# Where TensorE does its other work within a half step: between the scores for the maximum and the scores for the exponent, instead of after both

## The chip, the cores and the metric

The kernel runs on one core of a Trainium2 chip. TensorE (PE) multiplies matrices into PSUM, VectorE (DVE) does reductions and elementwise work, ScalarE (ACT) does exponentials and copies, GpSimd (POOL) elementwise work and indirect transfers, SyncE (SP) issues the other transfers. The metric is the device time of one execution in microseconds (us), lower is better; of several runs the median counts.

## What is computed

```python
x = L0_attn_x                                  # 16 batches, 512 tokens, 128 features
mod = (_silu(L0_c) @ L0_wmod)                  # per batch: shift, scale and gate, twice
h = _layernorm(x) * (1 + ca) + sa
q, k, v = h @ Wq.T + bq, h @ Wk.T + bk, h @ Wv.T + bv          # 16 heads of 8
attn = softmax(q @ k.T / sqrt(8))              # per head 512 x 512
x = x + ga * ((attn @ v) @ Wo.T + bo)
h = _layernorm(x) * (1 + cb) + sb
gating = softmax of the two best of 8 experts' scores (h @ gate_w.T)
x = x + gb * sum over the two experts of gating * (silu(h @ wg.T) * (h @ wu.T)) @ wd.T
```

## The kernel before

The attention of the 16 batches comes first, and the mixture of experts behind it, tile by tile. Each engine has one instruction stream, written out by hand and joined to the others by semaphores. A batch `b` is 16 slots `k = 0..15`; four slots make a group `g` of four heads, `hh = k % 4` is the slot within its group, and each slot has two halves, so that a batch has 32 half steps. Each half step handles 1024 scores in each of 128 rows (two heads of 512), twice:

- **Scores for the maximum** (line 824, tile `ps<-k_st,q_st`): two matmuls, for the group that is two groups ahead. DVE takes the row maximum of them (line 1331, `maxes`, one TENSOR_REDUCE a half step).
- **Scores for the exponent** (line 833, `ps<-q_st,k_st`): two matmuls, transposed, for the present group, with the negated maxima as two extra rows of the contraction. ACT takes exp of them into `probs` (line 1039, one ACTIVATE a half step).

PSUM has three areas of two banks for these, taken in turn by both kinds. So the scores for the exponent of half step s may be written when DVE has finished the maximum of half step s-1 (semaphore `maxes_done`), and the scores for the maximum of half step s when ACT has finished the exponent of half step s-2 (`exps_done`).

Once a slot TensorE also multiplies `probs` of the group before with `v_aug` (line 847, four matmuls of float32 that the trace counts as eight, into the bank `PV_BANK`): the **v_aug products**. In the first slot of a group they wait until ACT has copied the last group's result out of that bank (line 1046, `o_aug`, semaphore `pv_taken`); ACT does this copy after the first exponent of the group's first slot. Here `L111` rows in a listing are register arithmetic for the semaphore values inside a loop.

**Other steps** (`misc_at`, names in quotes) go through one shared bank, each filled by TensorE and drained by ACT or DVE before the next is filled: "shift" (the maxima transposed, line 757, drained by DVE at line 1177, then sent by DMA into `q_st`), "o" (line 762, drained at 1182 and 1184), "v" (753), "oT" (765), "y" (768, drained by ACT into `z`, line 1028, which waits for the small transfer of `prm_t`), "x1" (771), "hT" (746), "q" (748), "k" (750), "h2T" (775, waits for the second norm on POOL), "score" (778) and "where" (788 to 792) of the router, and "count" once. In a slot of the kernel before TensorE does: maximum, exponent, maximum, exponent, the first other step if there is one, the v_aug products, the second other step.

DVE has two reductions in a slot, and between them, at places written in the tables `NORM_AT` and `ROUTER_AT`, the small steps of the second layer norm and of the router. POOL splits q and k of the batch after next into three bfloat16 parts (lines 1515 to 1521) when ACT has drained "q" and "k" (line 1018), then does the second norm (1531 to 1538) and the scatters (1545). SP stores the parts of k to DRAM, and loads them back rearranged as `q_st` and `k_st` (line 518), behind which stand the loads of `x_r` and `prm_t` (488, 489). The new stacks are first read at k = 8. The last slots of batch 16 on, without any scores (`LATE`), are interleaved with the first tiles of the experts.

## Time and profile before

| | |
|---|---|
| median of 3 runs | 1455.21 us (1453.88 to 1474.65) |
| the profiled execution | 1465.6 us, its span 1463.7 us |
| mean granted TensorE clock | 0.879 of full speed |
| busy TensorE, DVE, ACT, POOL | 1097.3, 978.5, 784.1, 528.8 us |
| row maxima (line 1331), 512 times | 613.6 us, 1219 ns each |
| exponents (line 1039), 512 times | 523.1 us, 1023 ns each |
| first and last maximum | 51.5 and 1151.9 us |
| first and last exponent | 72.3 and 1177.3 us |

The span runs from the first to the last instruction; the whole execution is 1.9 us longer. The profiled execution took 0.7% more than the median of the other runs. The attention fills the time from about 51 to 1178 us, the experts fill the rest. Busy shares are means over both.

### The profile page before, as it was taken

To read this page: it belongs to the slowest core of one execution; us is meant where nothing else is said; L and a number is where in the kernel's file an instruction comes from. 1 tells how busy PE (TensorE), PEld (TensorE's weight loads), DVE (VectorE), ACT (ScalarE), POOL (GpSimd) and SP (SyncE) were. 2 spreads that over 40 slices of the span, in tenths; PEclk is the share of its full clock that TensorE was granted. 3 is DMA by queue.
4 is the path that set the end of the run, shared out by engine and by line. 5 is a ranking of instruction groups with operands and counts; after the bars stand their busy time and mean duration, and the time that the engine had idled before them with its cause. 6 is when DMAs were issued, how large, how long until landed. Compare 5 with 4: busy or idle time off the path is not lost.

```text
span 1463.7 us, 24448 instructions
## 1 busy us (share of the span) xinstructions
PE 1097.3 (75%) x6826; PEld 481.6 (33%) x6827; DVE 978.5 (67%) x2158; ACT 784.1 (54%) x1228; POOL 528.8 (36%) x591
## 2 busy tenths in 40 slices
PE   4477777767776878777877776878777788899981
PEld 2112222222222222222222222222222268798981
DVE  7567778686767675768675867675768554445555
ACT  3256756565555555555454655555555655455540
POOL 3112031423142323241405142323142157787754
PEclk9669999798789887889688989897889899999996
DMA  8132130314031212030303031213030042335677
GB/s 246 48 98 68 41 107 13 116 33 124 12 117 41 87 40 87 29 99 19 108 12 116 12 116 40 87 33 94 14 107 22 17 111 75 102 96 150 188 193 199
DMA packets 143146, 121.46 MB, mean 83 GB/s; under 512 B 20709, under 2 KB 133458, under 8 KB 139986
## 3 DMA queue, kind: packets, MB, share of 16 engines
q1 hardware_dynamic: 134354, 102.50, 24.4%
q0 software_dynamic: 8704, 17.97, 3.7%
q8 instruction: 32, 0.52, 0.1%
q14 instruction: 56, 0.46, 0.1%
HBM read 66.07 MB, written 53.76 MB: 82 GB/s over the span
## 4 chain that ended last, share of the span: by engine, by line
PE 47%; DVE 23%; issue 11%; DMA 6%; POOL 4%; SPq 4%; ACT 4%; DVEq 0%; ACTq 0%; POOLq 0%
PE ps L847 18%; DVE maxes L1331 17%; PE ps L833 6%; PE ps L824 4%; PE ps L896 3%; PE ps L762 3%; PE ps L913 2%; POOL ys_d L1584 2%; DMA k_st<-k_parts_d 2%; ACT probs L1039 2%; PE ps L768 1%; PE ps L905 1%; PE ps L748 1%; ACT o_aug L1046 1%; PE ps L778 1%
## 5 line engine op out<-in xcount | busy, mean ns | idle before, releaser
L1331 DVE TENSOR_REDUCE maxes<-ps 128x2 f32<-128x1024 f32 x512 | 613.6, 1219 | 177.4 <-PE ps L824 157.1
L1039 ACT ACTIVATE probs<-ps 128x1024 f32<-128x1024 f32 x512 | 523.1, 1023 | 342.9 <-PE ps L833 342.2
L833 PE MATMUL ps<-q_st,k_st 50*128 50x512 bf16 x1024 | 219.1, 427 | 253.3 <-DVE maxes L1331 236.6
L847 PE MATMUL ps<-probs,v_aug 128*32 128x512 f32 x2048 | 321.1, 704 | 13.4 <-ACT o_aug L1046 13.3
L1515 POOL TENSOR_TENSOR q_parts<-q,one 128x512 bf16<-128x512 f32 x16 | 16.6, 1035 | 713.0 <-ACT q L1018 713.0
L824 PE MATMUL ps<-k_st,q_st 48*128 48x512 bf16 x1024 | 224.5, 436 | 23.1 <-DMA k_st<-k_parts_d 18.9
L833 PEld LDWEIGHTS ps<-q_st,k_st 50*128 50x128 bf16 x1024 | 50.8, 97 | 405.4 <-DVE maxes L1331 375.3
L1545 POOL DMA_INDIRECT xs_d<-h,rows_o x128 | 123.4, 964 | 36.9 <-issue 36.3
L1460 DVE COPY probs<-ps 88x256 f32<-88x256 f32 x144 | 60.4, 419 | 100.7 <-PE ps L905 93.8
L824 PEld LDWEIGHTS ps<-k_st,q_st 48*128 48x128 bf16 x1024 | 53.3, 101 | 181.8 <-issue 95.4
L913 PE MATMUL ps<-wd_t,probs 88*128 x576 | 93.6, 286 | 0.1
L1584 POOL DMA_INDIRECT ys_d<-probs,k_st x72 | 71.2, 988 | 24.5 <-ACT probs L1096 11.9
L913 PEld LDWEIGHTS ps<-wd_t,probs 88*128 88x128 f32 x576 | 76.9, 194 | 4.8 <-issue 0.7
L1584 POOL DMA_INDIRECT ys_d<-probs,q_st x72 | 70.7, 981 | 17.8 <-POOL gone L1583 7.4
L896 PE MATMUL ps<-wg_t,probs 128*128 x288 | 73.2, 336 | 2.8 <-DVE probs L1464 2.2
L1086 ACT COPY probs<-ps 128x128 f32<-128x128 f32 x143 | 37.9, 265 | 67.2 <-PE ps L889 65.7
L847 PEld LDWEIGHTS ps<-probs,v_aug 128*32 128x32 f32 x2048 | 43.6, 114 | 76.5 <-issue 55.9
L896 PE MATMUL ps<-wu_t,probs 128*128 x288 | 67.7, 317 | 0.0
L905 PE MATMUL ps<-ident,probs 128*88 128x128 f32 x288 | 56.4, 278 | 9.9 <-DVE probs L1464 8.9
L1182 DVE RECIPROCAL o_rs<-ps 128x16 f32<-128x16 f32 x64 | 16.5, 258 | 65.2 <-PE ps L762 65.2
L762 PEld LDWEIGHTS ps<-ident,o_aug 128*128 128x128 f32 x256 | 32.9, 165 | 67.9 <-issue 57.5
L1464 DVE TENSOR_TENSOR probs<-probs,ps 128x176 f32<-128x176 f32 x144 | 46.5, 323 | 10.2 <-ACT probs L1090 9.8
(209 smaller groups left out, 1398.4 us busy)
## 6 DMA issues: line engine op xcount, KB each, us to landing
q_st<-q_parts_d SPq DMA_DIRECT2D x32, 384.0 KB
k_st<-k_parts_d SPq DMA_DIRECT2D x32, 384.0 KB
q_parts_d<-q_parts SPq DMA_DIRECT2D x16, 384.0 KB, 2.6
k_parts_d<-k_parts SPq DMA_DIRECT2D x16, 384.0 KB
probs<-ys_d SPq DMA_DIRECT2D x24, 256.0 KB, 4.8
...
```

The lines of the kernel that those rows point to most:

```text
L762: mm = pe.transpose(misc[:, P * t:P * (t + 1)], o_aug[g % 2][:, P * t:P * (t + 1)], ident[:, :])
L824: mm = pe.matmul(ps[:, 2 * area_of(2 * step) + side, :], q_st[bs % 2][rows, js, P * t:P * (t + 1)], k_st[bs % 2][rows, js, :], start=True, ...
L833: mm = pe.matmul(ps[:, 2 * area_of(2 * step + 1) + side, :], k_st[b % 2][rows, j, P * t:P * (t + 1)], q_st[b % 2][rows, j, :], start=True, ...
L847: mm = pe.matmul(ps[VW * i:VW * (i + 1), PV_BANK, :], v_aug[bp % 2][:, hh, GROUP * gp + i, :], probs[:, gp % 2, i, S * hh:S * (hh + 1)], s ...
L896: mm = pe.matmul(ps[:, GU_BANK + m % 2, INTER * i:INTER * (i + 1)], x_t[m % 2], w[:, :, :].rearrange("p c h -> p (c h)")[:, bass.ds(e * IN ...
L905: mm = pe.transpose(ps[0:HALF, HT_BANK, P * i:P * (i + 1)], hid[m % 2][:, HALF * i:HALF * (i + 1)], ident[:, :])
L913: mm = pe.matmul(ps[:, Y_BANK + m % 2, 0:D], hid_t[m % 2][:, P * i:P * (i + 1)], wd_t[:, bass.ds(e * 2 + i, 1), :].rearrange("p a d -> p ( ...
L1039: act.activation(probs[:, g % 2, pair_at:pair_at + 2, S * t:S * (t + 1)], ps[:, 2 * area:2 * area + 2, :], ACT.Exp, scale=SCALE).then_inc( ...
L1331: dve.tensor_reduce(maxes[g % 2][:, :, hh // 2, tile:tile + 1], ps[:, 2 * area:2 * area + 2, :], AX.X, ALU.max).then_inc(maxes_done, 1)
L1460: dve.tensor_copy(hid_t[(m - 1) % 2], ps[0:HALF, HT_BANK, 0:2 * P]).then_inc(hidt_taken, 1)
L1545: pool.indirect_dma_start(xs_d, bass.IndirectOffsetOnAxis(ap=rows_o[:, v:v + 1], axis=0), h2[n % 2][:, v // QT, v % QT, :], None).then_inc ...
L1584: pool.indirect_dma_start(ys_d, bass.IndirectOffsetOnAxis(ap=x_in[m % SLOTS][:, D + 1:XW].bitcast(U32), axis=0), y_out[m % SLOTS], None).t ...
```

## The change

In each half step TensorE now does the scores for the maximum, then one piece of other work, then the scores for the exponent. The two halves of a slot divide the pieces: the v_aug products in one half (the second in a group's first slot, the first in the other three), the other steps in `half` 0 or 1. "score" moves from k = 6 to k = 8, "where" from 13 to 12, "count" from 12 to 14. ACT and DVE drain in the order of the halves: ACT drains a step ahead of the exponent of the same half, DVE behind the maximum of the same half. `ROUTER_AT` moves the router's first 14 steps six places later and its last 13 four places earlier, and `LATE` is two slots shorter.

```diff
-LATE = [(NB, k) for k in range(GROUP, NH)] + [(NB + 1, k) for k in range(NH)] + [(NB + 2, k) for k in range(2)]
+LATE = [(NB, k) for k in range(GROUP, NH)] + [(NB + 1, k) for k in range(NH)]
-COUNT_AT = (NB - 1, 12)
+COUNT_AT = (NB - 1, 14)
...
-    if not end and (b, k) == COUNT_AT:
-        step = ("count", 0, 1)
-    elif not end:
-        step = {4: ("h2T", b - 2, NB), 6: ("score", b - 2, NB), 13: ("where", b - 2, NB)}.get(k)
+    if not half:
+        step = ("count", 0, 1) if (b, k) == COUNT_AT else {
+            4: ("h2T", b - 2, NB), 8: ("score", b - 2, NB), 12: ("where", b - 2, NB)}.get(k)
...
                             mm.then_inc(scores_ready, 1)
+                        if half == (hh == 0):
+                            weigh_values(b, g, hh, d)
+                        misc_steps(b, k, half, d)
                         if exps:
...
                             mm.then_inc(st_ready, 1)
-                        if half == 1:
-                            misc_steps(b, k, 0, d)
-                    if 0 <= s - 1 < NS:
...
-                        if hh == QT - 1:
-                            mm.then_inc(pv_ready, 1)
-                    misc_steps(b, k, 1, d)
+
+            def weigh_values(b, g, hh, d):
...
```

On ACT, and on DVE:

```diff
                     for half in range(2):
                         t, step = 2 * (hh % 2) + half, 2 * k + half
+                        other = misc_at(b, k, half)
+                        if other and other[0] in ("hT", "q", "k", "v", "oT", "y", "h2T"):
+                            misc_drain(*other, d)
                         if 0 <= s < NS:
...
-                    step = misc_at(b, k, 1)
-                    if step and step[0] in ("hT", "q", "k", "v", "oT", "y"):
-                        misc_drain(*step, d)
...
-            ROUTER_AT = ([BATCH_TILES + 27 + i for i in range(14)]
-                         + [BATCH_TILES + 53 + i for i in range(13)])
+            ROUTER_AT = ([BATCH_TILES + 33 + i for i in range(14)]
+                         + [BATCH_TILES + 49 + i for i in range(13)])
```

On TensorE, an inner slot of a group (k = 5 of a batch), before:

```order
L824 MATMUL ps<-k_st,q_st 128x512 [waits exps_done]
L824 MATMUL ps<-k_st,q_st 128x512
L833 MATMUL ps<-q_st,k_st 128x512 [waits maxes_done]
L833 MATMUL ps<-q_st,k_st 128x512
L824 MATMUL ps<-k_st,q_st 128x512 [waits exps_done]
L824 MATMUL ps<-k_st,q_st 128x512
L833 MATMUL ps<-q_st,k_st 128x512 [waits maxes_done]
L833 MATMUL ps<-q_st,k_st 128x512
L847 MATMUL ps<-probs,v_aug 32x512 x4
L762 MATMUL ps<-ident,o_aug 128x128 [waits pv_taken,misc_drained]
L762 MATMUL ps<-ident,o_aug 128x128 x3
```

and the same slot now (line 825 is the old 824, 837 the old 833, 852 the old 847, 763 the old 762):

```order
L825 MATMUL ps<-k_st,q_st 128x512 [waits exps_done]
L825 MATMUL ps<-k_st,q_st 128x512
L852 MATMUL ps<-probs,v_aug 32x512 x4
L837 MATMUL ps<-q_st,k_st 128x512 [waits maxes_done]
L837 MATMUL ps<-q_st,k_st 128x512
L825 MATMUL ps<-k_st,q_st 128x512 [waits exps_done]
L825 MATMUL ps<-k_st,q_st 128x512
L763 MATMUL ps<-ident,o_aug 128x128 [waits pv_taken,misc_drained]
L763 MATMUL ps<-ident,o_aug 128x128 x3
L837 MATMUL ps<-q_st,k_st 128x512 [waits maxes_done]
L837 MATMUL ps<-q_st,k_st 128x512
```

The v_aug products and the "o" transposes have moved from behind the second scores for the exponent to ahead of the first and of the second.

On TensorE, the first slot of a group (k = 4), from its first scores for the exponent on, before:

```order
L833 MATMUL ps<-q_st,k_st 128x512 [waits maxes_done,shift_stacked]
L833 MATMUL ps<-q_st,k_st 128x512
L824 MATMUL ps<-k_st,q_st 128x512 [waits exps_done]
L824 MATMUL ps<-k_st,q_st 128x512
L833 MATMUL ps<-q_st,k_st 128x512 [waits maxes_done]
L833 MATMUL ps<-q_st,k_st 128x512
L775 MATMUL ps<-ident,h_0 128x128 [waits h2_ready,misc_drained]
L775 MATMUL ps<-ident,h_0 128x128 x3
L847 MATMUL ps<-probs,v_aug 32x512 [waits misc_drained,pv_taken,exps_done]
L847 MATMUL ps<-probs,v_aug 32x512 x3
L757 MATMUL ps<-identb,shift 32x128 [waits shift_ready,misc_drained]
```

and the whole of that slot now:

```order
L825 MATMUL ps<-k_st,q_st 128x512
L776 MATMUL ps<-ident,h_0 128x128 [waits h2_ready,misc_drained]
L776 MATMUL ps<-ident,h_0 128x128 x3
L837 MATMUL ps<-q_st,k_st 128x512 [waits maxes_done,shift_stacked]
L837 MATMUL ps<-q_st,k_st 128x512
L825 MATMUL ps<-k_st,q_st 128x512 [waits exps_done]
L825 MATMUL ps<-k_st,q_st 128x512
L852 MATMUL ps<-probs,v_aug 32x512 [waits misc_drained,pv_taken,exps_done]
L852 MATMUL ps<-probs,v_aug 32x512 x3
L758 MATMUL ps<-identb,shift 32x128 [waits shift_ready,misc_drained]
L837 MATMUL ps<-q_st,k_st 128x512 [waits maxes_done]
L837 MATMUL ps<-q_st,k_st 128x512
```

"h2T" stands ahead of the first scores for the exponent, and the wait for `pv_taken` ahead of the second.

On ACT, at the end of slot 7 and the start of slot 8, before:

```order
L1006 ACTIVATE x_n<-x_a,prm_a 128x128 [waits misc_filled]
L111 REGISTER_ALU
L111 REGISTER_ALU [waits misc_filled]
L1028 ACTIVATE z<-ps,prm_t 128x512 [waits xr_loaded]
L111 REGISTER_ALU
L1039 ACTIVATE probs<-ps 128x2x512 [waits st_ready]
L111 REGISTER_ALU
L111 REGISTER_ALU [waits pv_ready]
L1046 COPY o_aug<-ps 128x512 [waits misc_filled]
```

and now (1032 is the old 1028, 1046 the old 1039, 1010 the old 1006, 1053 the old 1046):

```order
L1032 ACTIVATE z<-ps,prm_t 128x512 [waits xr_loaded]
L111 REGISTER_ALU
L1046 ACTIVATE probs<-ps 128x2x512 [waits st_ready]
L111 REGISTER_ALU
L111 REGISTER_ALU [waits xa_loaded]
L1010 ACTIVATE x_n<-x_a,prm_a 128x128 [waits misc_filled]
L111 REGISTER_ALU
L1046 ACTIVATE probs<-ps 128x2x512 [waits st_ready]
L111 REGISTER_ALU
L111 REGISTER_ALU [waits pv_ready]
L1053 COPY o_aug<-ps 128x512 [waits misc_filled]
```

The drain of "y", with its wait for a transfer, now stands ahead of the last exponent of slot 7.

## Rows read from the trace of the kernel before

**Rows 1.** The waits, 324.8 to 1058.6 us and 300 to 1000: total, times, longest.

```profile
PE ps L833 <- DVE maxes L1331: 160.1, 157, 5.5
DVE maxes L1331 <- PE ps L824: 99.1, 63, 3.2
...
DVE maxes L1331 <- issue: 16.5, 8, 2.6
```

**Rows 2.** ACT's copy of "k", and two stretches from one such copy to another.

```profile
L1018 ACT ACTIVATE k<-ps,bias x16: 687/687/688, 24.1 to 1058.6; 128x512 f32<-128x512 f32 x16
324.80:1058.60 733.80, 554.03 (x3242) 171.79 (x3240) 512.98 (x1002) 402.62 (x481) 221.54 (x211) 0.85 0.21 65
132.60:191.90 59.30, 42.99 (x304) 12.79 (x306) 45.69 (x73) 39.58 (x46) 8.90 (x9) 1.00 0.25 70
```

**Rows 3.** The timeline, one inner slot (k = 5): start, length, engine, line, idle before.

```profile
565.85 0.39 PE L824 MATMUL ps<-k_st,q_st 48*128 48x512 bf16 x2
...
566.08 0.38 PE L833 MATMUL ps<-q_st,k_st 50*128 50x512 bf16 x2
...
566.28 2.36 DVE L1331 TENSOR_REDUCE maxes<-ps 128x2 f32<-128x1024 f32 x2
...
566.50 1.02 ACT L1039 ACTIVATE probs<-ps 128x1024 f32<-128x1024 f32 x1 [0.94 <-PE ps L833]
...
567.57 0.39 PE L833 MATMUL ps<-q_st,k_st 50*128 50x512 bf16 x2 [0.89 <-DVE maxes L1331]
...
567.88 1.06 PE L847 MATMUL ps<-probs,v_aug 128*32 128x512 f32 x8
...
568.88 0.66 PE L762 MATMUL ps<-ident,o_aug 128*128 128x128 f32 x4
...
569.47 0.39 PE L824 MATMUL ps<-k_st,q_st 48*128 48x512 bf16 x2
```

**Rows 4.** The timeline: the copy at a group's start, and "v", the longest step.

```profile
560.83 1.16 PE L753 MATMUL ps<-w_t,h_t 128*128 128x128 f32 x8
...
600.26 0.58 ACT L1046 COPY o_aug<-ps 128x512 f32<-128x512 f32 x1
...
600.99 1.07 PE L847 MATMUL ps<-probs,v_aug 128*32 128x512 f32 x8 [0.40 <-ACT o_aug L1046]
```

**Rows 5.** Busy us (instructions) of PE, PEld, DVE, ACT, POOL; clock; DMA.

```profile
582.20:617.60 35.40, 27.58 (x161) 8.37 (x160) 26.41 (x63) 20.48 (x25) 3.06 (x3) 0.85 0.04 12
...
558.30:572.60 14.30, 10.77 (x78) 4.34 (x75) 10.41 (x13) 9.40 (x11) 4.79 (x5) 0.98 0.35 116
572.60:582.30 9.70, 9.22 (x34) 2.43 (x36) 3.38 (x9) 3.31 (x5) 0.00 (x0) 0.50 0.00 1
```

**Rows 6.** The same stretch for the row maxima alone (DVE, clock, DMA).

```profile
582.20:617.60 35.40, 19.20 (x16) 0.85 0.04 12
```

**Rows 7.** The timeline around a fall of the clock, TensorE.

```profile
571.67 1.36 PE L778 MATMUL ps<-gw_t,h_t 128*128 128x8 f32 x8
...
576.27 0.63 PE L833 MATMUL ps<-q_st,k_st 50*128 50x512 bf16 x2
576.70 0.63 PE L824 MATMUL ps<-k_st,q_st 48*128 48x512 bf16 x2
...
578.34 1.94 PE L847 MATMUL ps<-probs,v_aug 128*32 128x512 f32 x8
580.21 2.08 PE L768 MATMUL ps<-o_t,w_t 128*128 128x512 f32 x2
```

**Rows 8.** From "k" to the stacks: timeline, landing of `prm_t` (min, median, max).

```profile
692.08 0.69 ACT L1018 ACTIVATE k<-ps,bias 128x512 f32<-128x512 f32 x1 [1.10 <-PE ps L750]
...
696.78 1.16 POOL L1521 TENSOR_TENSOR k_parts<-rest,k_parts 128x512 bf16<-128x512 f32 x1
...
705.87 0.36 SPq L489 DMA_DIRECT2D prm_t<-prm_d x1
...
DMA to landing us min/median/max: 2.5/14.6/16.5
```

45 lines of the change are left out of this document (23 added, 22 removed).

## The prediction

> **What bounds the kernel now.** I read the page first for the shares, then the waits over ten steady batches, then the timeline of single slots, then the granted clock stretch by stretch. No engine is full: the ten batches between the copies of "k" take 733.8 us, 73.4 a batch, and in them TensorE is busy for 554 us and DVE for 513 [rows 2]. The waits show that the two wait for each other: TensorE stands 160.1 us for a row maximum before scores for the exponent, and DVE stands 99.1 us for TensorE before a maximum [rows 1]. One slot shows how. The scores for the maximum start at 565.85, the reduction at 566.28 (0.43 later), and the second scores for the exponent, which need its area, only at 567.57; TensorE stands 0.89 us. Only then come the v_aug products (1.00 us, 567.88 to 568.88) and the "o" transposes (0.59), and the next scores for the maximum start at 569.47. DVE has finished its two reductions at 568.64 and has nothing to read until 569.9 [rows 3]. So a slot is a loop: reduction 1.24, scores, products, other step, scores, 3.62 us for this one, although TensorE has only 4 x 0.22 + 1.00 + 0.59 = 2.5 us of work in it and DVE 2 x 1.18 = 2.4 and a drain.
>
> **The change, an inner slot.** Nothing is removed or added; each product takes what it took. The products and the other step now stand where TensorE waited. With a pair of scores at 0.22 (566.08 less 565.85 is 0.23) the order is scores 0.22, products 1.00, scores 0.22, scores 0.22, step 0.1 to 1.1, scores 0.22: 2.0 to 3.0 us. Three loops remain. DVE: 2.36 for two reductions, plus small steps. TensorE: those 2.0 to 3.0. ACT: scores for the exponent to the start of the exponent 0.42 (566.08 to 566.50), the exponent 1.02 [rows 3], release 0.05, the next scores for the maximum 0.22, then the products 1.00 before the next scores of that half: 2.7. A step that ACT drains adds its drain ahead of the exponent; "k" takes 0.69 [rows 2]. I take 2.75 for a slot with a short step and 3.1 for one with the longest ("v", 1.16 with its tail) [rows 4].
>
> **A group's first slot.** Here the products wait for the `o_aug` copy, which follows the first exponent. Before, TensorE was waiting for a maximum at that time anyway, so that only 0.40 us showed [rows 4]. Now the wait is in front of the second scores for the exponent. Counted from the first scores for the exponent: 0.42 + 1.02 + 0.58 (the copy) + 0.05, products 1.00, "shift" 0.15, scores 0.22 = 3.45 until the next scores for the maximum, 3.9 until DVE has something to reduce. The first slot also has to wait for the last maximum of the group before. Laid end to end in that way, a group of four slots with few small DVE steps comes to 3.5 + 2.5 + 2.9 + 3.2 = 12.1 us, and one with "h2T", "oT" and "y" to 12.9, since "h2T" is drained ahead of that exponent. The first half of a batch: **25 us**. Queued behind the waiting products are the "shift" transposes and the scores; who waits for them is DVE. A price for the wait from both sides: 0.40 as now, or all of the 2.07 us from scores to the copy's end; I use the second less what DVE still has to reduce.
>
> **The second half of a batch** (k = 8 to 15) is where the router's and the norm's small steps lie. DVE was busy for 26.4 us of it, 19.2 of them in 16 reductions [rows 5, 6], so the 47 others took 7.2, 0.15 each. The new table moves 7 more router steps in (those at k = 6 and 7, and in the next batch's slot 0): 7 x 0.15 = 1.1. That is 27.5 us of DVE, which is now the bound; two group starts leave it idle for 0.65 us each, and dependent steps and POOL's splits running beside it add some 2: **31 us**. "score" and "where" move to a group's first slot, where their 1 us stands beside the wait for the last maximum and costs nothing; if that wait were gone they would cost 2 us a batch.
>
> **Transfers.** They keep their length while the slots get shorter. "k" was drained at 692.08, POOL's split of it ended at 697.94, and `prm_t`, last in the row behind the stacks, was issued at 705.87 and takes 14.6 us: 28.4 us after "k" [rows 8]. SP was held there by a "shift" drain which will come earlier; I work out 27.2. "y" is drained at k = 7, some 24 us after "k", and ACT has to have `prm_t` for it, now ahead of an exponent: a wait of 2 to 3 us, which delays the second scores of k = 8: **2 us** a batch. Bounds: 0 (in the few batches with a quick landing, 2.5 us) and 4.4 (all of 28.4). The stacks themselves land just before k = 8 on that count. POOL's second norm, which "h2T" at k = 4 waits for, is five operations of about a split's 1.16 [rows 8] behind the split: 6 us more, some 11 us after the batch's start where 12.1 is early enough. No cost, with 1 us to spare.
>
> **Once a loop turn**, of two batches, DVE waits for its own instructions, 16.5 us in five turns [rows 1]: **1.5 us** a batch, unchanged.
>
> **The clock.** At the low level, 1.2 GHz against 2.4, products take 1.87 (578.34 to 580.21) and a pair 0.43 [rows 7]. The mean of 0.85 over the ten batches means 30% of the time at the low level [rows 2]. It fell at 572.6 right after "score", eight columns a matmul, though TensorE had been busy for 10.8 of the 14.3 us before, at 0.98, and it rose 9.7 us later [rows 5, 7]. A slot without other work needs 4 x 0.43 + 1.87 = 3.6 us there, with one 4.6 to 5.5, so TensorE is the bound and a slot costs some 1.2 more than laid out above. With TensorE a little denser, but "score" and "where" next to the new waits, I take a quarter of the time: about three slots, **3.5 us**. The Trainium skill speaks against this term: "TensorE: Matmul & The Clock Gate", section "What's actually happening", lets the clock fall only after an idle window. By that rule the term would be near 0. The trace does not agree: what precedes the fall at 572.6 is three quarters work.
>
> **The sum.** 25 + 31 + 2 + 1.5 + 3.5 = 63 us a batch against 73.4: 10.4 saved in each of ten batches, 104. The three batches ahead of them (192.2 us from 132.6 to 324.8, 64.1 each) have less DVE work and a clock of up to 1.00 [rows 2]: 7.3 each, 22. Batch 0's last eight slots and batches 14 and 15: 17. The start is bound by transfers and the experts' part by its own steps; the two LATE slots less let the second map be made two tiles earlier, which nobody waits for: 0. In all 143 us of the profiled execution's 1465.6, 1322.6; the median stood 0.7% below that execution, so **1313 us**.
>
> **Rivals.**
> *A, the clock stays up.* If a denser TensorE keeps 2.4 GHz, the 3.5 us go too: 14 x 3.5 = 49 less, 1264. This is what the Trainium skill's rule on idle windows, named above, would give. For it: the batch from 132.6 to 191.9 ran at 1.00 throughout. Against: that batch has no "score" and no "where".
> *B, ACT becomes the bound.* Steps are drained ahead of exponents, and copies stand before products. If each of eight drains a batch (0.7) delays the loop in full, it costs 5.6 us, less what is in the slots above: 69 a batch, 1313 + 14 x 6 = 1397. For it: the ACT loop of 2.7 is longer than DVE's 2.36. Against: ACT was busy for 403 of 734 us [rows 2].
> *C, the clock stays down: slower.* At 1.2 GHz throughout, a batch is 16 x 3.6 = 57.6 of scores and products and twice 10.5 of other steps (at the full clock four "shift" of 0.15, four "o" of 0.59, ten others of 0.6 to 1.1), 80 us with the loop turn: 6.6 more than now, 1455 + 14 x 6.6 = 1547. It would come about if new waits, at each group's start and before k = 8, make the clock fall again whenever it has risen. It decides against the change when the low level holds for (73.4 - 59.5) / (80 - 59.5) = 68% of the time, against 30 now. Against: total waiting shrinks.
> *D, nothing gained.* The moved work doesn't lie under the wait, because something else ends last at each scores for the exponent: POOL's chain from "k" through split, store and load to k = 8 stretches with the traffic. To hold a batch at 73 it would have to take 10 us more than the 28.4 seen: 1455.
>
> **Chances.** The forecast, with batches of 61 to 66 us, 0.45; A 0.22; B, or a transfer that waits by some us more, 0.20; C 0.06; D 0.07. A measurement of this kernel tells about 2% from no change. Faster by over 2%: 0.45 + 0.22 + 0.20 less a little for a weak B = 0.86; within 2% 0.08; slower 0.06. The range takes in A with a batch at 57.5 us, the bare sum of both halves and the loop turn (1313 - 14 x 5.5 = 1236), and B (1397) with a little for a longer wait at k = 8: 1235 to 1405.
>
> **What the profile after would show.** Batches of about 63 us between copies of "k". TensorE's wait for maxima before scores for the exponent down to a third of 160; DVE's wait for scores mostly at group starts, about 1 us each. A new wait of the products for `o_aug`, 1.3 to 1.6 us, 60 times. ACT waiting for `prm_t` before `z` for 2 to 3 us a batch. A clock of 0.86 to 0.92. The time of one product, reduction and exponent unchanged. I am wrong if the clock's mean leaves these bounds, if ACT's queue holds the exponents longer, or if the stacks come after their slot.

## The result

| | before | after |
|---|---|---|
| median of 4 runs | 1458.72 us (1453.88 to 1474.65) | **1400.58 us** (1395.41 to 1405.94) |
| profiled execution, its span | 1465.6, 1463.7 us | 1395.4, 1393.6 us |
| mean granted TensorE clock | 0.879 | 0.853 |

The ratio is **0.9584, 95% interval 0.9497 to 0.967**: faster by 58 us of medians (70.1 us between the two spans), where 143 were forecast. Here and below a median counts all runs, while a ratio is formed from the runs in the faster of the two states in which a kernel is found, and no clock is given for e7 and e10, whose profiled executions fell in the slower one. The reduction now has line 1332, and the other steps keep their tiles.

The page of the changed kernel: busy time of the engines, and two of the costliest groups.

```profile
PE 1113.4 (80%) x6826; PEld 477.0 (34%) x6827; DVE 981.3 (70%) x2158; ACT 779.6 (56%) x1228; POOL 528.5 (38%) x591
...
L1332 DVE TENSOR_REDUCE maxes<-ps 128x2 f32<-128x1024 f32 x512 | 622.3, 1222 | 136.5 <-PE ps L825 119.3
L852 PE MATMUL ps<-probs,v_aug 128*32 128x512 f32 x2048 | 341.9, 746 | 78.4 <-ACT o_aug L1053 63.5
```

The counts and the length of a reduction are as before. What changed is who waits. The products (line 852) now stand 63.5 us for the `o_aug` copy over the whole run. The stretches between copies of "k" (columns as in [rows 2]):

```profile
129.60:185.90 56.30, 46.57 (x304) 12.97 (x304) 45.82 (x74) 39.14 (x46) 8.93 (x9) 0.94 0.25 74
315.90:982.90 667.00, 548.37 (x3242) 164.03 (x3242) 513.77 (x1003) 399.88 (x480) 221.37 (x211) 0.83 0.24 72
```

The copies themselves, in the timeline grouped by tile (how many; shortest, middle and longest in ns; first and last start):

```profile
L1022 ACT ACTIVATE k<-ps,bias x14: 687/687/688, 129.6 to 982.9; 128x512 f32<-128x512 f32 x14
```

Ten batches take 667.0 us where [rows 2] had 733.8: 66.7 each instead of 73.4, with the same instructions (x3242 on TensorE) and a mean clock of 0.83 instead of 0.85. TensorE was idle for 179.8 us of them before (733.80 less 554.03) and is for 118.6 now. The time of the whole went like this:

| stretch | before | after | saved | forecast |
|---|---|---|---|---|
| start to the copy of "k" at 129.6 | 132.6 | 129.6 | 3.0 | 0 |
| three batches | 192.2 | 186.3 | 5.9 | 22 |
| ten batches | 733.8 | 667.0 | 66.8 | 104 |
| the rest | 405.1 | 410.7 | -5.6 | 17 |

The waits in the ten batches (total, times, longest), to be set beside [rows 1]:

```profile
DVE maxes L1332 <- PE ps L825: 64.1, 114, 1.7
DVE shift_t L1178 <- PE ps L758: 57.7, 32, 2.4
...
PE ps L852 <- ACT o_aug L1053: 39.8, 31, 1.6
...
PE ps L837 <- DVE maxes L1332: 22.4, 20, 4.0
PEld ps L789 <- DVE top L1241: 18.7, 10, 1.9
...
PE ps L789 <- DVE top L1241: 13.7, 10, 1.4
...
ACT z L1032 <- DMA prm_t<-prm_d: 5.2, 3, 2.8
```

TensorE's wait for a maximum fell from 160.1 to 22.4 us. The main mechanism is there. Two other waits of TensorE have come up: 39.8 us for `o_aug`, 31 times and up to 1.6 us (forecast at each group's start; 6.7 us before), and 13.7 for `top`, 1.4 us each time, once a batch. The second is not in the prediction at all. Line 789 is "where"; its weight load (PEld) waits 1.9 us.

DVE's wait for scores fell from 99.1 to 64.1 us, but the one for "shift", which TensorE now does behind the waiting products, rose to 57.7. In the same ten batches before it was:

```profile
DVE shift_t L1177 <- PE ps L757: 20.2, 29, 1.7
```

**An inner slot and a group's first slot.** The timeline of TensorE over k = 4 and the beginning of k = 5 (start, length):

```profile
605.74 0.39 PE L837 MATMUL ps<-q_st,k_st 50*128 50x512 bf16 x2
606.01 0.39 PE L825 MATMUL ps<-k_st,q_st 48*128 48x512 bf16 x2
607.97 1.07 PE L852 MATMUL ps<-probs,v_aug 128*32 128x512 f32 x8 [1.57 <-ACT o_aug L1053]
608.85 0.22 PE L758 MATMUL ps<-identb,shift 128*32 128x128 bf16 x1
609.00 0.39 PE L837 MATMUL ps<-q_st,k_st 50*128 50x512 bf16 x2
609.22 0.38 PE L825 MATMUL ps<-k_st,q_st 48*128 48x512 bf16 x2
609.53 1.06 PE L852 MATMUL ps<-probs,v_aug 128*32 128x512 f32 x8
610.53 0.39 PE L837 MATMUL ps<-q_st,k_st 50*128 50x512 bf16 x2
610.76 0.38 PE L825 MATMUL ps<-k_st,q_st 48*128 48x512 bf16 x2
611.07 0.65 PE L763 MATMUL ps<-ident,o_aug 128*128 128x128 f32 x4
611.66 0.39 PE L837 MATMUL ps<-q_st,k_st 50*128 50x512 bf16 x2
612.04 0.39 PE L825 MATMUL ps<-k_st,q_st 48*128 48x512 bf16 x2
```

The slot of k = 5 runs from 609.22 to 612.04, 2.82 us, with hardly a gap (the forecast was 2.75; [rows 3] had 3.62). At k = 4 the products wait 1.57 us for the copy; from the first scores for the exponent, 605.74, to the next scores for the maximum, 609.22, it is 3.48 us (forecast 3.45). Both units of the sum were right. What the 3.45 leaves out is what stands ahead of the first scores for the exponent.

**The slot of k = 8**, where "score" (line 779) has been put:

```profile
616.84 1.23 DVE L1332 TENSOR_REDUCE maxes<-ps 128x2 f32<-128x1024 f32 x1 [0.31 <-PE ps L825]
...
618.80 1.06 PE L779 MATMUL ps<-gw_t,h_t 128*128 128x8 f32 x8 [0.41 <-ACT z L1032]
619.79 0.39 PE L837 MATMUL ps<-q_st,k_st 50*128 50x512 bf16 x2
```

The last reduction of the group before ends at 618.07, so there is no wait for a maximum left to hide anything under. "score" waits 0.41 us for ACT's drain of "y" and takes 0.99, and the scores for the exponent start right behind it. From the scores for the maximum, which start at 618.01, it is 1.78 us to them. At k = 4 it is the same with "h2T": scores for the maximum 604.49, last reduction over at 604.52, "h2T" from 605.16 on, scores for the exponent 605.74.

**The slot of k = 12** is the surprise. The timeline of three engines:

```profile
632.03 0.38 PE L825 MATMUL ps<-k_st,q_st 48*128 48x512 bf16 x2
...
633.59 0.14 DVE L1241 TENSOR_TENSOR top<-top 128x4 f32<-128x4 f32 x1
...
633.79 0.64 PE L789 MATMUL ps<-route,tri 128*128 128x32 f32 x2 [1.37 <-DVE top L1241]
...
634.24 1.43 PE L791 MATMUL ps<-route,ones 128*128 128x24 f32 x6
...
635.52 0.61 PE L793 MATMUL ps<-before,ones 128*128 128x32 f32 x2
...
636.07 0.61 PE L837 MATMUL ps<-q_st,k_st 50*128 50x512 bf16 x2
...
636.72 1.02 ACT L1046 ACTIVATE probs<-ps 128x1024 f32<-128x1024 f32 x1 [3.45 <-PE ps L837]
...
638.36 1.93 PE L852 MATMUL ps<-probs,v_aug 128*32 128x512 f32 x8 [1.26 <-ACT o_aug L1053]
```

After the scores for the maximum (632.03) TensorE comes to "where", whose input is the router's step on DVE that ends at 633.73. It stands 1.37 us for it, then "where" takes 2.3 us, and only then (636.07) come the scores for the exponent, which ACT had been waiting for since 633.3. Its `o_aug` copy is thereby late as well, and the products wait another 1.26. The clock, as stretches from the same place:

```profile
604.00:632.00 28.00, 23.75 (x169) 7.77 (x170) 22.88 (x41) 21.49 (x28) 1.92 (x2) 1.00 0.16 55
632.00:634.00 2.00, 0.63 (x5) 0.21 (x2) 2.00 (x8) 1.15 (x2) 0.00 (x0) 0.83 0.00 0
634.00:642.00 8.00, 6.74 (x31) 2.84 (x35) 4.42 (x15) 2.56 (x4) 0.00 (x0) 0.50 0.01 2
```

It was 1.00 (2.4 GHz) until 632, through the wait at k = 4 too. The 0.83 of the next 2.00 us means the low level for their last 0.7, so it fell at about 633.3, while TensorE stood for `top` (until 633.79); then it is 0.50 (1.2 GHz) for at least 8 us.

**Mean slot lengths.** From scores for the maximum to the next, worked out from the timeline and averaged over the ten batches (k = 0 has the loop turn in it):

| k | 0 | 1 | 2 | 3 | 4 | 5 | 6 | 7 | 8 | 9 | 10 | 11 | 12 | 13 | 14 | 15 |
|---|---|---|---|---|---|---|---|---|---|---|---|---|---|---|---|---|
| before | 6.6 | 5.4 | 3.6 | 4.2 | 3.9 | 3.6 | 6.2 | 5.3 | 3.6 | 3.8 | 3.9 | 5.3 | 3.6 | 5.4 | 4.8 | 4.2 |
| after | 7.1 | 4.3 | 2.9 | 3.2 | 5.3 | 3.3 | 2.8 | 3.3 | 5.8 | 3.2 | 2.8 | 3.4 | 8.4 | 4.0 | 3.1 | 3.6 |

The twelve slots that don't begin a group gained 15.6 us a batch, and the four that do (0, 4, 8, 12) lost 8.8. The net 6.8 is what the stretches show.

### The profile page after: what moved, and what is told of

Read it like the earlier page. It is cut to its first block, busy times and chain, and to the rows that moved or that the text cites. A ratio compares the mean times of both kernels' runs of the same rounds, so it can differ in the third digit from the quotient of the medians.

```text
span 1393.6 us, 24448 instructions
## 1 busy us (share of the span) xinstructions
PE 1113.4 (80%) x6826; PEld 477.0 (34%) x6827; DVE 981.3 (70%) x2158; ACT 779.6 (56%) x1228; POOL 528.5 (38%) x591
## 4 chain that ended last, share of the span: by engine, by line
PE 41%; issue 16%; DMA 12%; DVE 11%; SPq 6%; ACT 6%; POOL 6%; DVEq 1%; ACTq 0%; POOLq 0%
PE ps L852 15%; PE ps L837 7%; DMA prm_t<-prm_d 5%; DVE maxes L1332 5%; PE ps L825 5%; ACT probs L1046 3%; PE ps L900 3%; PE ps L917 2%; POOL ys_d L1584 2%; DMA k_st<-k_parts_d 2%; ACT o_aug L1053 2%; PE ps L763 2%; DMA k_parts_d<-k_parts 1%; PE ps L909 1%; PE ps L779 1%
## 5 line engine op out<-in xcount | busy, mean ns | idle before, releaser
L1332 DVE TENSOR_REDUCE maxes<-ps 128x2 f32<-128x1024 f32 x512 | 622.3, 1222 | 136.5 <-PE ps L825 119.3
L852 PE MATMUL ps<-probs,v_aug 128*32 128x512 f32 x2048 | 341.9, 746 | 78.4 <-ACT o_aug L1053 63.5
L1460 DVE COPY probs<-ps 88x256 f32<-88x256 f32 x144 | 60.4, 420 | 101.1 <-PE ps L909 93.5
L1178 DVE COPY shift_t<-ps 32x128 bf16<-32x128 bf16 x64 | 13.5, 211 | 91.3 <-PE ps L758 90.9
L1531 POOL TENSOR_TENSOR h<-x_s,ln 128x512 f32<-128x512 f32 x16 | 16.6, 1039 | 89.2 <-DMA row<-row_d 48.0
```

The lines of the kernel that those rows point to most:

```text
L852: mm = pe.matmul(ps[VW * i:VW * (i + 1), PV_BANK, :], v_aug[bp % 2][:, hh, GROUP * gp + i, :], probs[:, gp % 2, i, S * hh:S * (hh + 1)], s ...
L1332: dve.tensor_reduce(maxes[g % 2][:, :, hh // 2, tile:tile + 1], ps[:, 2 * area:2 * area + 2, :], AX.X, ALU.max).then_inc(maxes_done, 1)
L1460: dve.tensor_copy(hid_t[(m - 1) % 2], ps[0:HALF, HT_BANK, 0:2 * P]).then_inc(hidt_taken, 1)
```

## The experiments

"A batch" is the distance of the thirteen copies of "k" divided by 13 (71.2 us before, 65.6 after). Ratios are to the kernel before on the same chip.

| run | edit | median | ratio [95%] | a batch | clock |
|---|---|---|---|---|---|
| e1_router_early | after + router two steps a place | 1365.4 | 0.9425 [0.9335, 0.9514] | 63.8 | 0.873 |
| e2_copy_early | after + `o_aug` copy early | 1329.7 | 0.9185 [0.9137, 0.9232] | 61.4 | 0.884 |
| e3_prm_early | after + `x_r`, `prm_t` ahead of the stacks | 1405.9 | 0.971 [0.9636, 0.9785] | 66.4 | 0.848 |
| e4_drain_behind | after + ACT drains behind the exponent | 1448.2 | 0.9987 [0.9942, 1.0033] | 69.1 | 0.831 |
| e5_router_copy | e1 and e2 together | 1306.8 | 0.8946 [0.8871, 0.902] | 60.0 | 0.892 |
| e6_products_only | before + only the products moved | 1382.4 | 0.9484 [0.9396, 0.9573] | 64.6 | 0.903 |
| e7_before_copy_early | before + copy early | 1440.4 | 0.9856 [0.9772, 0.994] | 70.8 | |
| e8_router_copy_prm | e5 + `prm_t` alone ahead | 1314.8 | 0.8984 [0.887, 0.9097] | 60.4 | 0.889 |
| e9_steps_only | after, products back at the slot's end | 1336.3 | 0.9187 [0.9093, 0.9281] | 61.9 | 0.913 |
| e10_router_copy_xr | e5 + both loads a batch ahead | 1280.9 | 0.8723 [0.8608, 0.8839] | 58.9 | |
| e11_old_places | after with the tables of before | 1420.5 | 0.9749 [0.9652, 0.9847] | 66.9 | 0.851 |
| e12_filled_waits | after + useless matmuls in the `o_aug` wait | 1401.7 | 0.963 [0.9532, 0.9727] | 65.7 | 0.866 |
| e13_steps_router | e9 + e1 (disturbed, see there) | 1485.8 | 0.9451 [0.9373, 0.9529] | 68.0 | 0.859 |
| e14_steps_copy | e9 + copy early (beside e13) | 1436.7 | 0.9127 [0.906, 0.9194] | 64.0 | 0.880 |
| e15_steps_all | e10, products at the end (beside e13) | 1438.3 | 0.9139 [0.9079, 0.92] | 64.6 | 0.873 |
| e16_all_one_chip | e10 again | 1271.6 | 0.8764 [0.8691, 0.8837] | 58.2 | 0.901 |
| e17_steps_all_one_chip | e15 again, beside e16 | 1291.4 | 0.8898 [0.8822, 0.8974] | 59.5 | 0.926 |
| e18_steps_router_copy | e17, loads in their old place | 1302.4 | 0.8957 [0.8865, 0.9049] | 60.1 | 0.916 |

### The wait of "where" for the router (e1)

```diff
-            ROUTER_AT = ([BATCH_TILES + 33 + i for i in range(14)]
+            ROUTER_AT = ([BATCH_TILES + 33 + i // 2 for i in range(14)]
...
-                        if place in ROUTER_AT:
-                            router_step(ROUTER_AT.index(place), n, d)
+                        for i, p in enumerate(ROUTER_AT):
+                            if p == place:
+                                router_step(i, n, d)
```

> The changed kernel, with the router's first 14 steps two to a place (places 33 to 39 of the batch in place of 33 to 46), so that the last of them is done on DVE long before TensorE reaches "where" at k = 12. Theory 1, group starts: the changed kernel loses in the first slot of a group what it gains in the others (k = 12 takes 8.4 us where it took 3.6 before), and part of that is the 1.9 us that the weight load of "where" waits for DVE's step 13 (L1241). Then k = 12 drops to about 6.5 and a batch by 2 us: 1373 us, ratio to the kernel before 0.941. Theory 2, clock: "where" makes the clock fall wherever it stands, the slot stays above 7.5 and the whole moves by under 10 us (ratio 0.952 or more).

35 us less than the changed kernel by medians, 23 by the two ratios. No wait for `top` is left; slot 12 went from 8.4 to 5.9 us and the clock up. The wait for `o_aug` is untouched, as the waits of e1 between 310 and 960 us show:

```profile
PE ps L852 <- ACT o_aug L1053: 39.8, 29, 1.6
```

So the wait of "where" costs 2.5 us in its slot, and 1.8 a batch, since slots 8 to 10 got a little longer. With the wait gone slot 12 is still 2.3 us longer than before (5.9 against 3.6): "where" itself and the wait for `o_aug` stand in it.

### The wait of the products for `o_aug` (e2, e5, e12, e7)

e2 lets ACT copy behind the first exponent of a group's last slot, in which the products end; the products then no longer find the bank full.

```diff
-                        if hh == 0 and half == 0 and 0 <= s - 2 < NS:
+                        if hh == GROUP - 1 and half == 0 and 0 <= s - 1 < NS:
...
-                            wait(act, pv_ready, lambda b: NG * b + g - 1, b, d)
+                            wait(act, pv_ready, lambda b: NG * b + g, b, d)
...
-                            act.copy(o_aug[g % 2][:, :], ps[:, PV_BANK, :]).then_inc(pv_taken, 1)
+                            act.copy(o_aug[(g + 1) % 2][:, :], ps[:, PV_BANK, :]).then_inc(pv_taken, 1)
```

> The changed kernel, with ACT's copy of the v_aug products (o_aug) behind the first exponent of a group's last slot, where the products are finished, in place of behind the first exponent of the next group's first slot. Theory 1, group starts: the products' wait for that copy, 1.3 to 1.6 us at each group start, goes; what is late next is the last maximum of the group before, 0.3 to 0.5 us behind it. Some 1 us for each of 60 groups: 1340 us, ratio 0.92. Theory 2, clock: the waits are what makes the clock fall, so its mean rises over 0.88 as well and the time is 1325 or less. Rival, transfers: the batch is held by the chain from k through split, store and load (prm_t is on the chain that ended last for 5% of the span); the slots only wait elsewhere, and the time stays above 1385.

71 us less than the changed kernel by medians, 58 by the ratios: the k = 4 slot went from 5.3 to 3.1 us. Something else then came up. The waits of e2 between 310 and 960 us:

```profile
ACT z L1032 <- DMA prm_t<-prm_d: 25.8, 9, 7.3
...
PE ps L825 <- DMA k_st<-k_parts_d: 18.3, 8, 6.5
```

These are the transfers that the prediction spoke of; slots 7 and 8 (5.0 and 5.7 us on average) are where they are waited for. e5 puts e1's and e2's edits together.

> The changed kernel with both edits: the router's first 14 steps two to a place, and the o_aug copy behind the first exponent of a group's last slot. Theory 1, group starts: the two losses are separate (1.9 us before "where", 1.1 us for each of 60 groups) and add up: 0.9425 and 0.9185 against the change's 0.9584 give 0.9584 - 0.016 - 0.040 = 0.903, 1317 us. Rival, transfers: with the copy early alone k = 7 and 8 already wait for prm_t and for the stacks (4.7 and 5.2 us a slot), and what the router's edit gives comes out there again: 0.915 or more.

94 us less than the changed kernel (93 by the ratios). The sum of the two is 106 by medians and 81 by ratios: two separate waits, that add up. 1306.8 us is near the 1313 that had been forecast for the change itself.

e12 asks whether the wait costs by itself or through the clock: it leaves the wait and fills it with five matmuls of 48 rows, whose result nobody reads.

```diff
+                        if hh == 0 and half == 1 and exps and 0 <= s + 1 < NS:
+                            wait(pe, misc_drained, lambda b: at["shift", NG * b + g + 1], b, d)
+                            for _ in range(5):
+                                pe.matmul(misc, k_st[b % 2][0:SHIFT, j, P * t:P * (t + 1)], q_st[b % 2][0:SHIFT, j, :],
+                                          start=True, stop=True)
                         if half == (hh == 0):
                             weigh_values(b, g, hh, d)
```

> The changed kernel with five useless bf16 matmuls of 48 rows by 512 columns into the shared bank before the products in each group's first slot, where TensorE waits 1.3 to 1.6 us for the o_aug copy; 1.1 us of work at the high clock. It computes nothing new; the bank is written again by "shift". Theory 2, the new waits make the clock fall: its mean rises from 0.853 to 0.89 or more and 15 to 40 us go, ratio 0.93 to 0.95. Theory 1, what is lost is the waits themselves and the clock falls at "score" and "where", with few active columns: the mean stays below 0.87, the time within 1% of the changed kernel or up to 10 us longer.

The visible wait is nearly gone (3.6 us in 12 times), slots 4 and 5 stayed at a steady 4.7 and 2.8 us, and the mean clock rose from 0.853 to 0.866. The time did not move (0.963 against 0.9584, with intervals that overlap): slot 12 remained (9.2 us), and the five matmuls take more than the wait wherever the clock is low, 2.34 us at 771.64 against 1.25 at 805.70. So the higher clock alone brought nothing here; how the cost of the wait divides between waiting and clock isn't shown, since the filling adds work of its own.

e7 is the control: the copy early in the kernel before (there `half == 1`, since the products stand at the slot's end).

> The kernel before with the o_aug copy behind the second exponent of a group's last slot. Theory 1: the wait for this copy is new in the changed kernel; before, TensorE stood at most 0.4 us for it, 6.7 us in ten batches, so 5 to 10 us at most go: ratio 0.993 to 1. Rival: the place of the copy is worth much in either order (it keeps ACT free at the group's start): 0.98 or less.

18 us by medians, 21 by the ratio (0.9856, interval 0.977 to 0.994): between the two expectations, and more than the kernel before shows as waiting, 6.7 us in ten batches. The 0.40 us of [rows 4] is one of the long ones, not the mean of 60. Why the copy's place is worth more than its wait stays open. Of what e2 gave back about a third was thus to be had without the change, and the rest goes with the change's own wait.

### The transfers (e3, e8, e10)

e3 moves `load_x_r(b - 1, d)`, the loads of `x_r` and `prm_t`, ahead of `store_parts` and `load_stacks` in SP's stream:

```diff
+                if 0 <= b - 1 < NB:
+                    load_x_r(b - 1, d)
                 if b + 1 < NB:
...
-                if 0 <= b - 1 < NB:
-                    load_x_r(b - 1, d)
```

> The changed kernel, with SP's loads of x_r and prm_t ahead of the stores of k's parts and the loads of the stacks, so that the drain of "y" never waits for prm_t. Theory 1: that wait is 7.2 us in all, so 0 to 10 us less: 1390 to 1401. Rival, transfers: the chain that ended last runs through prm_t for 5% of the span (70 us), and if it really sets the batch, 20 us or more go (1380 or less). It may also cost, if the 256 KB of x_r ahead delay the stacks past k = 8: then a wait of the scores for the maximum for stack_ready appears in the trace.

No gain: in the changed kernel `z` waited only 5.2 us in ten batches, and the stacks, now later, were waited for instead (8.3 us for `k_st` between 310 and 960 us, where the changed kernel has 1.5). e8 repeats it where the transfers do bind, on top of e5, with `prm_t` alone ahead and `x_r` left behind the stacks:

```diff
             def load_x_r(n, d):
 
+                b = batch_of(n, d)
+                sp.dma_start(x_r[:, :, :], x[b].rearrange("(t p) d -> p t d", p=P)).then_inc(xr_loaded, 16)
+
+            def load_prm_t(n, d):
+
                 wait(sp, misc_drained, lambda n: at["x1", n - 1] + 1 if n else 0, n, d)
                 b = batch_of(n, d)
-                sp.dma_start(x_r[:, :, :], x[b].rearrange("(t p) d -> p t d", p=P)).then_inc(xr_loaded, 16)
                 sp.dma_start(prm_t[:, :], prm_d[b]).then_inc(xr_loaded, 16)
...
+                if 0 <= b - 1 < NB:
+                    load_prm_t(b - 1, d)
                 if b + 1 < NB:
```

> The kernel of e5 with SP's small load of prm_t (6 KB) ahead of the stores of k's parts and of the stacks, x_r left behind them. ACT's wait for prm_t before z (25.8 us in 650 with the copy early) goes. Theory, transfers bind only through prm_t: 20 to 30 us less than e5, about 1295. Rival: the stacks land 2 us later than prm_t is wanted, the wait moves from z to the scores for the maximum at k = 8, and under 12 us are gained.

No gain over e5 (0.8984 against 0.8946). The waits of e8 between 310 and 960 us:

```profile
ACT z L1039 <- DMA x_r<-L_attn_x: 23.9, 11, 8.2
...
PE ps L832 <- DMA k_st<-k_parts_d: 17.2, 8, 7.7
```

The semaphore counts both loads, and the last in the row behind the stacks is the late one, whichever it is. e10 issues both a batch earlier, behind `store_x1` and `load_row` of the batch before, as soon as "x1" has freed them:

```diff
-                if 0 <= b - 1 < NB:
-                    load_x_r(b - 1, d)
...
                     load_row(b - 1, d)
+                if 0 <= b < NB:
+                    load_x_r(b, d)
```

> The kernel of e5 with x_r and prm_t loaded a batch earlier, behind the store of x1, where no other transfer runs, in place of behind the stacks. Theory, what is last in the row behind the stacks lands late (with prm_t moved ahead alone, z waited for x_r in its place): z's waits of 25.5 us go, and the scores for the maximum at k = 8 become what waits, for k_st, 1 to 3 us a batch. 10 to 25 us less than e5: 1290, ratio 0.883. Rival: both waits are one chain (from k through split and stacks), nothing is gained: 0.89 or more.

The fastest kernel of the study, 1280.9 us, and 1271.6 as e16. Both loads now land 3.6 us after their issue at the median (3.5 and 3.6 in e16), and `z` waits for no transfer any more. The stacks are still waited for in some batches: 7.6 us in all between 310 and 880 us of e16, up to 6.2 at a time.

### The two halves of the change apart (e6, e9), and ACT's order (e4)

e6 is the kernel before with nothing changed but the products' place: `weigh_values` is called behind the scores for the maximum, in the halves that the change uses.

```diff
                             mm.then_inc(scores_ready, 1)
+                        if half == (hh == 0):
+                            weigh_values(b, g, hh, d)
                         if exps:
```

> The kernel before with one part of the change: only the v_aug products move, to between the scores for the maximum and for the exponent; the other steps, their drains, the tables and LATE stay as they were. Theory 1: inner slots lose the 1.0 us of the products from their loop (3.25 to about 2.4 without another step, 3.62 to 2.9 with "o"), the first slot of each group gains the wait for o_aug (+1.2 us), "where" stands behind the second scores as before and does not wait for DVE: about 12 x 0.8 - 4 x 1.2 = 4.8 us a batch less, 1385 us, ratio 0.95, no worse than the whole change. Rival, that the other steps' place carries most of the gain: 0.975 or more.

The waits of e6 between 310 and 960 us:

```profile
PE ps L853 <- ACT o_aug L1051: 56.3, 35, 2.1
...
PE ps L835 <- DVE maxes L1336: 32.7, 60, 2.9
```

It gains as much as the whole change, with a larger wait for `o_aug`. e9 is the opposite: the steps moved, the products back at the slot's end.

```diff
-                        if half == (hh == 0):
-                            weigh_values(b, g, hh, d)
                         misc_steps(b, k, half, d)
...
                             mm.then_inc(st_ready, 1)
+                    weigh_values(b, g, hh, d)
```

> The changed kernel with the v_aug products back behind the slot's last scores for the exponent; the other steps stay between the two kinds of scores, the tables are the new ones. Theory 1, the products carry the change and bring its loss with them: inner slots keep the products in their loop (3.2 us each, and nothing more for a step), group starts have no wait for o_aug, k = 12 keeps the wait of "where". 12 slots of 3.3 and 4 group starts of about 4.4, two of them 1 to 3 longer, and 1.5 for the loop turn: 64 to 68 us a batch, ratio 0.94 to 0.97. Rival, each part gives half: 0.975 to 0.985.

The waits of e9 between 310 and 930 us:

```profile
PE ps L835 <- DVE maxes L1331: 51.7, 79, 3.4
...
PE ps L851 <- ACT o_aug L1052: 19.7, 26, 1.0
...
PE ps L789 <- DVE top L1240: 2.7, 10, 0.3
```

A miss for both theories, on the good side: 0.9187. The wait for maxima is twice the changed kernel's, but that for `o_aug` is half and that for `top` a fifth. As built, moving the products as well costs 64 us (58 by the ratios).

e4 puts ACT's drains behind the exponent of the same half, the rest as changed (three lines moved behind the exponent):

```diff
-                        other = misc_at(b, k, half)
-                        if other and other[0] in ("hT", "q", "k", "v", "oT", "y", "h2T"):
-                            misc_drain(*other, d)
...
                                            ps[:, 2 * area:2 * area + 2, :], ACT.Exp, scale=SCALE).then_inc(exps_done, 1)
+                        other = misc_at(b, k, half)
+                        if other and other[0] in ("hT", "q", "k", "v", "oT", "y", "h2T"):
+                            misc_drain(*other, d)
```

> The changed kernel, with ACT's drains of the other steps behind the exponent of the same half step instead of ahead of it. Rival B of the prediction (drains ahead of exponents make ACT the bound): eight drains a batch of 0.6 to 0.8 us no longer stand before an exponent, a batch loses 3 us, 1360 or less. Theory 1: inner slots are bound by the loop over the exponent only in part; what is gained there (at most 0.5 us for each of the 8 slots) is lost where the next step waits for the shared bank ("score" behind "y", "h2T" behind "v"): 1390 to 1410.

The waits of e4 between 320 and 960 us:

```profile
PE ps L789 <- ACT h_t L1018: 14.8, 9, 1.6
...
PE ps L779 <- ACT z L1032: 13.8, 9, 1.6
...
PE ps L776 <- ACT v_aug L1025: 13.1, 9, 1.5
```

Both expectations missed: the whole gain was gone. A step drained behind the exponent comes late for the next step, which at k = 4, 8 and 12 stands in front of scores for the exponent ("h2T", line 776, "score", 779, and "where", 789; the three first slots take 7.4, 7.8 and 8.2 us). The drains ahead of the exponents are part of what makes the change pay.

### The tables (e11)

```diff
-            4: ("h2T", b - 2, NB), 8: ("score", b - 2, NB), 12: ("where", b - 2, NB)}.get(k)
+            4: ("h2T", b - 2, NB), 6: ("score", b - 2, NB), 13: ("where", b - 2, NB)}.get(k)
...
-            ROUTER_AT = ([BATCH_TILES + 33 + i for i in range(14)]
-                         + [BATCH_TILES + 49 + i for i in range(13)])
+            ROUTER_AT = ([BATCH_TILES + 27 + i for i in range(14)]
+                         + [BATCH_TILES + 53 + i for i in range(13)])
```

> The changed kernel with the tables of before: "score" at k = 6 and "where" at k = 13 (each in half 0, behind the products of that half), the router's steps at 27 and 53, LATE two slots longer; only the order within a half step is new. Theory 1: "where" no longer waits for DVE's step 13 nor stands before a group's first scores for the exponent, so k = 12 falls from 8.4 to about 5, k = 8 from 5.8 to 5, against some 1 us more at k = 13 and 1.5 at k = 6: 3 us a batch less, 1360, ratio 0.93. Rival, the tables belong to the order: "oT" behind "score" in k = 6 now waits for DVE's drain, k = 6 and 13 rise by 2 to 3 us each, and nothing is gained (0.955 or more).

Slot 12 falls from 8.4 to 5.4 us as theory 1 wanted, but slots 6, 7 and 13 rise by 2.6, 1.2 and 2.1, and nothing is gained (0.9749 against 0.9584), as the rival said. The old places don't suit the new order either.

### What the products' place is worth without its waits (e13 to e18)

e9 left a question: do the products cost by their place, or by the two waits? e13, e14 and e15 have the products at the slot's end, with e1's edit, with the early copy (`half == 1`), and with both and e10's loads.

> The changed kernel with the products put back to the slot's end (as the run with the steps alone, 0.9187) and the router's first 14 steps two a place. Theory 1 (where the products stand before the exponent scores, a late step waits twice: as a step and through the products queued behind it; with the products behind, a late step costs only itself): the router edit is worth less here than in the whole change, since 'where' at k = 12 showed no wait for 'top' with the products behind: at most 8 us, 1328 to 1336, ratio 0.912 to 0.919. Theory 2 ('where' ahead of the exponent scores costs by its being there, whatever the products do, and the router edit pays by making DVE's work denser): again 23 us, 1313, ratio 0.903.

> The changed kernel with the products put back to the slot's end and the o_aug copy moved behind the last exponent of the group before. With the steps alone the products' wait for o_aug was 19.1 us over ten batches and the kernel stood at 0.9187. Theory 1 (moving the products loses 4% through the o_aug wait alone; with the copy early the loss is gone and there is a gain left): little to win here, 10 us at most, 1325 to 1336, ratio 0.911 to 0.919, so behind the whole change with the copy early (0.9185 by itself, 0.8946 with the router's steps). Theory 2 (the products are better at the slot's end in any case, by the clock, whose mean was 0.91 there): the copy adds to it as it did in the whole change, 30 us or more, 1306 or less, ratio 0.898 or less.

> The best kernel so far (router's steps two a place, o_aug copy early, x_r and prm_t a batch ahead: 1280.9, 0.8723) with one difference: the products are back at the slot's end. This measures what the products' move is worth once its waits are gone. Theory 1 (they fill TensorE's wait for the maximum, as laid out in the prediction: inner slots 2.8 instead of 3.0): slower than 0.872 by 16 x 0.2 us a batch in 14 batches, some 45 us: 1325, ratio 0.90. Theory 2 (the other step in that place fills enough, and the products ahead of the exponent scores only lengthen ACT's loop and lower the clock): as fast or faster, 1245 to 1280, ratio 0.85 to 0.872.

In these three the kernel before itself took 1577 us beside them, and their traces have stalls of up to 7 us, mostly at k = 3 and 4, for which the profile names no engine of the core but "remote". The record has them and the next three under one chip number, 14, so whether it was another chip or a passing condition of the same one is not known. From the waits of e15 between 320 and 930 us:

```profile
DVE maxes L1331 <- remote: 49.1, 15, 6.8
...
ACT v_aug L1023 <- remote: 33.5, 6, 7.3
```

No other run shows such rows, so these three ratios say nothing beside the others, and nothing is concluded from them. The next three ran beside each other, with the kernel before at 1452 us and no such stalls.

> The fastest kernel once more (products ahead of the exponent scores, router's steps two a place, o_aug copy early, x_r and prm_t a batch ahead), beside its counterpart with the products at the slot's end. On the chip of the call before, the kernel before took 1577 us and showed stalls of 5 to 7 us that no other chip had, so that its ratios can't be set beside the others. Expected here: 0.872 again, if this chip is like the first ones.

> The same but for the products, which stand at the slot's end. In the disturbed run of this kernel the undisturbed slots k = 9 to 15 lasted 3.25, 4.29, 3.07, 4.02, 3.03, 3.68, 3.21 us, 24.6 in all, and the inner slots of the first half 3.03; with the products ahead of the exponent scores the latter are 2.82. Theory 1 (once the waits are gone the moved products pay, by the inner slots of the first half): slower than the other by 6 to 8 slots of 0.2 us in 14 batches, 17 to 25 us, a ratio higher by 0.012 to 0.017: 0.884 to 0.889. Theory 2 (the place itself costs, by the clock): a ratio lower than the other's by 0.01 or more.

> The products at the slot's end, router's steps two a place, o_aug copy early, the loads of x_r and prm_t in their old place: the counterpart of the run with the same two edits and the products ahead, which gave 0.8946. Theory 1: 0.905 to 0.915, a little above it, or equal if the transfers bind in both. Theory 2: 0.885 or less. Beside the run with everything it also says what the loads are worth while the products are at the slot's end: 1 to 2 per cent if the second half of a batch comes early enough to wait for them, nothing if not.

e16 and e17 differ by the place of the products and, with it, by the half of the group's last slot in which ACT copies `o_aug` (0 in e16, 1 in e17, behind the products in both). Their copies of "k", first e16's:

```profile
L1021 ACT ACTIVATE k<-ps,bias x14: 687/687/703, 123.8 to 879.8; 128x512 f32<-128x512 f32 x14
```

and e17's:

```profile
L1020 ACT ACTIVATE k<-ps,bias x14: 687/689/690, 124.7 to 897.9; 128x512 f32<-128x512 f32 x14
```

58.2 against 59.5 us a batch, 1271.6 (1267 to 1275) against 1291.4 us (1285 to 1293). Theory 1 had expected 17 to 25 us; it is 20. The place costs nothing by itself: once its waits are gone, the move pays. e18 with 0.8957 equals e5 (0.8946), and it would seem that there the transfers take back the gain: between 310 and 880 us `z` waits 7.7 us in e18 and 17.7 in e5.

## Why the prediction was right in direction and too low by 88 us

- **The mechanism and its units: right.** 160.1 us of waiting for maxima became 22.4 (a third was forecast). Inner slots 2.82 (2.75), with "v", "y" or "q" 3.13 to 3.17 (3.1), a group's start 3.48 (3.45). Reductions, exponents and products keep their length. e6 and e9 show that each half of the change pays alone. Of the 143 us forecast 73 are missing in the profiled execution: 37 in the ten batches, 16 in the three ahead of them, 20 at the two ends.
- **The step that failed first: "'score' and 'where' move to a group's first slot, where their 1 us stands beside the wait for the last maximum and costs nothing".** There is no such cover. At k = 8 the last reduction is over at 618.07 and the scores for the exponent start at 619.79, behind "score"; the slot went from 3.6 to 5.8 us. "where" is 2.3 us at 1.2 GHz, and what it needs itself was not asked. It waits 1.4 us (its weight load 1.9) for the router's step, and all of it stands ahead of the scores that a whole group waits for: slot 12 went from 3.6 to 8.4 us. e1 gives back 1.8 us a batch, 23 to 35 us in all. That the fallback in the same sentence said 2 us a batch is chance: it priced the steps themselves, and e1 removes a wait that the sentence does not have.
- **The price of a group's start.** I took 3.5 us for the whole of it and let DVE's remaining work hide a part. The 3.5 is right from the first exponent scores on, but 1.25 us at k = 4 ("h2T" and its wait for ACT) and 1.78 at k = 8 stand ahead of them: first slots are 4.7 to 5.0 us at the full clock, a group 13.5 to 13.8 instead of 12.1 and 12.9, and the first half of a batch 27.3 instead of 25 (shortest values of each slot in the ten batches, summed). e2 puts a size on the `o_aug` wait, which had been forecast as such: 58 to 71 us with what it brings along, of which e7 finds 18 to 21 without the change.
- **The second half** came to 31.2 us, in the same kind of sum, as forecast, but by errors that cancel, which is luck: its inner slots are not bound by DVE (2.8 us, where I had them longer by the small steps), and k = 12 takes what they leave.
- **The clock: 3.5 us a batch, forecast; 5 to 6.4, worked out from the trace.** 66.7 less 27.3, 31, 1.5 for the loop turn and 0.5 for transfers is 6.4, a remainder that holds all that varies from batch to batch. The mean of 0.83 means the low level for 34% of the time, not 25, which at the prediction's price makes 5.0. The mean over the whole, 0.853, lies below the 0.86 to 0.92 that the prediction had named, so this term is wrong by its own sign too. The clock was also lower in the three batches ahead (0.94, 0.89 and 0.80, where the kernel before had 1.00, 0.97 and 0.88), which goes, with their group starts, with their having given 5.9 us and not 22. I had noted that the new waits could do this, and gave it only to rival C. What makes the clock fall stays open. The Trainium skill ("TensorE: Matmul & The Clock Gate", section "What's actually happening") lets the clock fall after an idle window. The trace agrees only in that the fall shown above comes within a wait: TensorE had stood for 0.9 us of it and been busy for 23.75 of the 28 us before, and a longer wait (1.57 us, k = 4) left the clock at 1.00 in the same batch. The length of one wait does not say which it will be.
- **The transfers: 2 us a batch, forecast; 0.5, measured.** The slots stayed long. When e2 shortened them, the wait came as described, 25.8 us in nine times.
- **The ends: 17 us forecast, 2.6 lost.** This was only carried over from the steady batches. From the last copy of "k" to the start of the last exponent it is 120.7 us, where the kernel before took 118.7 (1058.6 to 1177.3), and from there to the end 290.0 instead of 286.4. The last exponents of the changed kernel and of e2:

```profile
L1046 ACT ACTIVATE probs<-ps x512: 1012/1023/1057, 74.0 to 1103.6; 128x1024 f32<-128x1024 f32 x171
L1046 ACT ACTIVATE probs<-ps x512: 1012/1023/1084, 74.5 to 1031.5; 128x1024 f32<-128x1024 f32 x171
```

  With its last copy of "k" at 927.5, e2 takes 104.0 us for the first of the two stretches, and e1 114.0 (959.4 to 1073.4). So the last batches lose by the same waits as the steady ones, and without the one for `o_aug` their gain is there (14.7 us). The 3.6 us at the very end stay open.
- **Rivals.** A (clock stays up) is refuted by 0.83. B (ACT's drains ahead of the exponents) named a time near the result, 1397, but not for the right reason: with a drain ahead of the exponent the inner slots kept to their forecast (2.82 with "oT", 3.13 to 3.17 with "v", "y" or "q"), and e4 brings no gain by moving the drains, but 48 us of loss through other waits. C needed 68% of the time at the low level; it was 34 in the ten batches. D did not happen.
- **What the whole is worth:** the change as made (0.958) is no better than the products' move alone (0.948) and worse than the steps' move alone (0.919). With the three waits removed that it opens (`top`, `o_aug`, the late loads) it is the best: 0.872 and 0.876, and its products' share is 20 us of that. How much of the 0.872 the old order would reach with the same three helps was not run, but for the copy (e7, 0.986).
